# A decoder layer on one core: the first attention layer gets memory of its own, and the cross layer's loop begins beside it at its step 25 in place of 38

## The chip, the cores and the metric

The kernel runs on one core of one Trainium2 chip. The metric is the device time of one execution in microseconds (us), as the median of several runs. The engines are named as the profile names them: PE (TensorE; PEld is its weight load), DVE (VectorE), ACT (ScalarE), POOL (GpSimd) and SP (SyncE, here a queue of DMA issues).

## The reference, cut to what matters

Eight batches of 112 tokens and 512 columns go through three layers, each with a layer norm ahead of it and a residual sum behind it.

```python
x = x + _L0_attn_ref(_layernorm(x), Wqkv_w, Wqkv_b)    # 16 heads of 32, rotary, causal, scores in float32
x = x + _L0_xattn_ref(_layernorm(x), ctx_2048, ...)    # a second layer norm, values rounded to fp8 steps,
                                                       # 16 heads over x and 16 over ctx (375 rows), projection
x = x + _L0_ffn_ref(_layernorm(x), w_gate_up, w_proj)  # ternary weights, silu gate
```

Below, the first line is called the A layer. The second is called the cross layer; its first half is attention over x itself (halves S0 and S1 of eight heads each), its second half attention over the context (X0 and X1). The quantities of the A layer that matter here are, for each batch: q, k and v from one product with a bias, scores and softmax of four groups of four heads, and the product with v; then the two layer norms of the cross layer and four quantised copies of their result, which the cross layer's products read.

## The kernel before, in words

Everything is written out by hand. Each call `pe(...)`, `dve(...)`, `act(...)` or `pool(...)` appends one instruction to that engine's list with the semaphore values that it waits for, so the order of the calls in Python is the order of each engine's queue. Two step loops make those calls.

**The A layer's loop** is `run_a`, a generator of 53 steps. In a step it goes through `plan`, a list of stages with the step at which the first batch comes to them; a batch follows every 4 steps. The stages of a batch are: layer norm statistics `a_ln` and its scaling `a_h`, transposes `a_tr`, three products `a_mm` (L455, 12 matmuls each, one per step in three of four steps), addition of the bias on DVE `a_ev` (L467), rotary on POOL `a_rotary` (L481 to L487), transposes of q and k `a_tq` (L495) and their copies `a_te`. Then come the groups of four heads, one per step and four per batch: `a_s0` (scores L520 and L523 on PE, row maximum L529 on DVE, four exponentials L532 on ACT), `a_s2` (transposes L546) one step later, `a_s3` (product with v, L570) another step later, and `a_s4` (division and residual sum on DVE, L586 to L594). Last come the cross layer's two norms, `l_0` to `l_2` (L649 transposes), and `l_q` with `quant`: one multiplication, three short DVE instructions (L609 to L612) and two on POOL (L613, L614), four times for each batch. The norms' reciprocal roots are four small POOL instructions (L374 to L377). The lag between a batch's first step and its first head group is `A_LEAD`, 10.

**The cross layer's loop** is the `while tick < ...` loop at the end: item after item of `proj_items` (products `p_mm`, L806, 8 matmuls; for q and k then statistics `p_stats` on DVE, L386, roots on POOL, `lnb_z` on ACT, L746, and transposes L757), and 8 steps behind it the items of `att_items` (`t_s0` to `t_s6`; L896, L940 and L975 on PE, quantisation by `quant`, and the projection L1013 once per batch). Background stages `b_0` and `b_1` split the weights of the next half into a high and a low bf16 part; S1's begin at step 15. Each step of this loop begins with one further step of `run_a`, as long as there is one.

Before the change, 38 steps of `run_a` are emitted by themselves and the last 15 inside the cross layer's loop. S0's weights are split during the 38 (`s0prep`, one piece a step from step 3). The limit of 38 comes from memory: the two layers share places. The A layer keeps q and k in `aKV`, where the cross layer keeps its keys and values (`kS`, `vS`), keeps its bias, softmax and transposed softmax in the attention rings of the cross layer, and shares `zr` with it. The code hands the places over with `free_rings`, which makes the first use of a ring wait until all engines have come to a given point.

Eight PSUM banks go round in a pool, `bank`; four staging slots for weights go round in `st_ring`.

## Time and profile before

| | |
|---|---|
| median of 3 runs | 1350.96 us (1349.79 to 1355.85) |
| time of the profiled execution | 1349.61 us |
| its span | 1347.8 us |
| busy: PE, DVE, ACT, POOL | 1224.5, 977.8, 727.2, 826.1 us |
| share of the span | 91%, 73%, 54%, 61% |
| last A step emitted by itself ends, cross layer's first product starts | 215 us |

The page cuts the span into 40 slices of 33.7 us. The A layer fills the first six or so, and the cross layer's attention over x the next ones. PE's busy time is modelled at its end and counts slow matmuls as busy too, so it is read together with the granted clock.

### The profile page before, as it was taken

To read this page: it belongs to the slowest core of one execution; us is meant where nothing else is said; L and a number is where in the kernel's file an instruction comes from. 1 tells how busy PE (TensorE), PEld (TensorE's weight loads), DVE (VectorE), ACT (ScalarE), POOL (GpSimd) and SP (SyncE) were. 2 spreads that over 40 slices of the span, in tenths; PEclk is the share of its full clock that TensorE was granted. 3 is DMA by queue.
4 is the path that set the end of the run, shared out by engine and by line. 5 is a ranking of instruction groups with operands and counts; after the bars stand their busy time and mean duration, and the time that the engine had idled before them with its cause. 6 is when DMAs were issued, how large, how long until landed. Compare 5 with 4: busy or idle time off the path is not lost.

```text
span 1347.8 us, 19252 instructions
## 1 busy us (share of the span) xinstructions
PE 1224.5 (91%) x6411; PEld 832.4 (62%) x6432; DVE 977.8 (73%) x2826; ACT 727.2 (54%) x1936; POOL 826.1 (61%) x1106
## 2 busy tenths in 40 slices
PE   3999998679999999999999999998889887798998
PEld 1666666456667666677777777765556555455545
DVE  3557886689988887577776666599999999564241
ACT  3444444567766765565555555576567656551130
POOL 1747885886786777344444453379778878465271
PEclk8888887999999999999999999999999999798999
DMA  8211100002220221011111111112221220000000
GB/s 245 64 48 47 32 1 1 0 1 64 63 64 1 64 85 53 27 40 55 51 43 55 55 47 32 32 35 63 75 59 51 67 66 16 1 1 5 24 1 28
DMA packets 18835, 59.30 MB, mean 44 GB/s; under 512 B 2240, under 2 KB 2368, under 8 KB 18736
## 3 DMA queue, kind: packets, MB, share of 16 engines
q1 hardware_dynamic: 17152, 55.03, 13.3%
q10 hardware_dynamic: 1584, 3.05, 0.8%
q8 instruction: 51, 0.84, 0.3%
q14 instruction: 48, 0.39, 0.1%
HBM read 56.23 MB, written 1.84 MB: 43 GB/s over the span
## 4 chain that ended last, share of the span: by engine, by line
PE 55%; DVE 26%; POOL 11%; ACT 4%; issue 2%; DMA 1%; ACTq 0%; POOLq 0%; SPq 0%
PE ps L816 11%; PE ps L1080 7%; PE ps L1013 7%; PE ps L806 5%; PE ps L455 4%; DVE big L928 4%; PE ps L975 4%; PE ps L1129 4%; PE ps L908 4%; POOL big L375 3%; DVE big L352 3%; PE ps L940 2%; DVE big L386 2%; PE ps L523 2%; DVE big L353 2%
## 5 line engine op out<-in xcount | busy, mean ns | idle before, releaser
L816 PE MATMUL ps<-big 128*125 128x512 bf16 x1152 | 267.3, 382 | 1.3 <-ACT big L911 1.2
L746 ACT ACTIVATE big<-ps,big 112x128 f32<-112x128 f32 (+1 forms) x512 | 192.5, 458 | 88.4 <-POOL big L377 87.7
L816 PEld LDWEIGHTS ps<-big 128*125 128x125 bf16 x1152 | 156.9, 138 | 82.9 <-issue 2.2
L374 POOL TENSOR_SCALAR big<-big 112x4 f32<-112x4 f32 (+2 forms) x160 | 46.7, 292 | 259.8 <-DVE big L389 254.5
L806 PE MATMUL ps<-big 128*112 128x512 bf16 x768 | 184.4, 383 | 4.6 <-ACT big L746 1.9
L375 POOL TENSOR_TENSOR big<-big 112x4 f32<-112x4 f32 (+2 forms) x160 | 161.1, 1007 | 13.5 <-DMA big<-in_cst 0.2
L928 DVE TENSOR_SCALAR big<-big 112x112 f32<-112x112 f32 (+1 forms) x256 | 158.4, 639 | 6.8
L911 ACT ACTIVATE big<-ps,big 112x375 f32<-112x375 f32 x128 | 74.1, 579 | 147.9 <-DVE big L910 147.8
L613 POOL TENSOR_TENSOR big<-big 128x448 f32<-128x448 bf16 x96 | 99.7, 1038 | 69.3 <-DVE big L925 53.4
L806 PEld LDWEIGHTS ps<-big 128*112 128x112 bf16 x768 | 99.6, 131 | 67.0 <-issue 5.1
L386 DVE BATCH_NORM_STATS2 big<-ps 112x6 f32<-112x128 f32 (+1 forms) x512 | 113.1, 282 | 37.7 <-PE ps L816 32.8
L975 PE MATMUL ps<-big 125*128 125x224 f32 (+1 forms) x512 | 123.3, 364 | 11.5 <-ACT big L955 10.8
L614 POOL TENSOR_TENSOR big<-big 128x448 bf16<-128x448 f32 x96 | 120.9, 1259 | 7.5
L1013 PE MATMUL ps<-big 128*112 128x512 bf16 x512 | 115.9, 380 | 2.7 <-POOL big L377 1.3
L975 PEld LDWEIGHTS ps<-big 125*128 125x128 f32 (+1 forms) x512 | 93.4, 196 | 23.5 <-ACT big L955 13.9
L908 PE MATMUL ps<-big 128*112 128x375 f32 x256 | 104.8, 491 | 2.8 <-ACT big L955 2.8
L1080 PE MATMUL ps<-big 128*128 128x448 bf16 x512 | 98.3, 353 | 0.0
L455 PE MATMUL ps<-big 128*112 128x512 bf16 x288 | 84.2, 454 | 14.9 <-DVE big L242 13.9
L940 PEld LDWEIGHTS ps<-big 112*125 112x125 f32 (+1 forms) x512 | 79.4, 178 | 27.6 <-ACT big L341 3.3
L763 ACT ACTIVATE big<-ps,big 128x448 f32<-128x448 f32 (+1 forms) x128 | 96.0, 750 | 0.3 <-PE ps L757 0.3
L1013 PEld LDWEIGHTS ps<-big 128*112 128x112 bf16 x512 | 65.6, 130 | 47.5 <-issue 4.4
L940 PE MATMUL ps<-big 112*125 112x112 f32 (+1 forms) x512 | 86.3, 271 | 8.9 <-ACT big L341 4.3
(113 smaller groups left out, 2365.4 us busy)
## 6 DMA issues: line engine op xcount, KB each, us to landing
big<-in_ctx_t SPq DMA_DIRECT2D x32, 375.0 KB, 3.1
big<-in_w_s SPq DMA_DIRECT2D x16, 512.0 KB, 3.6
big<-in_w_p SPq DMA_DIRECT2D x16, 512.0 KB, 3.6
big<-in_w_x SPq DMA_DIRECT2D x16, 512.0 KB, 3.6
big<-in_w_g SPq DMA_DIRECT2D x16, 512.0 KB, 4.1
big<-in_w_d SPq DMA_DIRECT2D x8, 512.0 KB, 3.6
big<-in_w_a SPq DMA_DIRECT2D x8, 384.0 KB, 4.5
big<-in_x ACTq DMA_DIRECT2D x8, 224.0 KB, 8.6
```

Of the source, the lines that this page charges most:

```text
L375: t = pool(lambda e: e.tensor_tensor(r, r, cf[0:rows, C_HALF:C_HALF + n], ALU.pow), t, t_c)
L386: t = dve(lambda e, j=j: e.bn_stats(st[:, j, :], src[0:rows, width * j:width * j + width]), toks, free)
L455: t = pe(lambda e, k=k, s=s, w=w, n=n: e.matmul(bk[0:T, :], xT[:, s, k, :], wA[:, w, k, 512 * j:512 * j + 512], start=n == 0, stop=n == 11 ...
L746: t = act(lambda e, j=j: e.activation(z[0:rows, 128 * j:128 * j + 128], bk[0:rows, 128 * j:128 * j + 128], ACT.Identity, bias=rr[0:rows, 4 ...
L806: t = pe(lambda e, k=k, s=s, n=n: e.matmul(bk[0:T, :], xq[:, k, :], w[:, s, k, col:col + 512], start=n == 0, stop=n == 7), xq_tok[(v, b)], ...
L816: t = pe(lambda e, k=k, s=s, u=u, n=n: e.matmul(bk[0:CK, :], cT[:, s, k, CK * c:CK * c + CK], w[:, u, k, col:col + 512], start=n == 0, sto ...
L908: t = pe(lambda e: e.matmul(bk[0:T, 0:SC], q[:, h, :], kk[:, g, :], start=True, stop=True), bt["ready"], free)
L928: tl = dve(lambda e, j=j: e.tensor_scalar(hl[0:T, w * j:w * j + w], p[0:T, w * j:w * j + w], ri[:, j:j + 1], None, ALU.mult), tr, hf)
L940: t = pe(lambda e, j=j: e.transpose(bb[0:rows, T * j:T * j + T], hl[0:T, rows * j:rows * j + rows], identf[0:T, 0:T]), it["tl"], free, sig ...
L975: t = pe(lambda e, c=c: e.matmul(bk[:, o:o + 224], v[0:rows, c, 128 * g:128 * g + 128], pT[0:rows, 224 * c:224 * c + 224], start=c == 0, s ...
L1013: t = pe(lambda e, h=h, s=s, n=n: e.matmul(bk[0:T, :], cat[:, h, :], hf["wp"][:, s, h, :], start=n == 0, stop=n == 15), bt["tcat"], free, ...
L1080: t = pe(lambda e, k=k, s=s, n=n, bk=bk, which=which: e.matmul(bk[:, 0:448], wg[:, k, 2048 * which + 128 * m:2048 * which + 128 * m + 128] ...
```

## The change

Memory. The A layer gets places that nothing of the cross layer's first half uses. Its bias and one shared ring `az` go into staging slots 2 and 3, which the A layer borrows until its end (`a_lent`), so that only two staging slots are left for the weights meanwhile. q and k go into the last part of the ring for transposed softmax (`aPT`), which the cross layer's first half leaves free; the rest goes into two areas inside PW[0], behind the A layer's own weights. To fit, some rings lose a slot: v 3 to 2, softmax 3 to 2, q and k 2 to 1 each, and one slot `az` takes the place of `zr`, `zl` and the old `az`. The bias is no longer loaded from ACT's queue at the start but from SP's, behind the A layer's weights.

Order. `A_LEAD` is 9 in place of 10; in a step `a_s3` comes first, and the transposes of q and of k both come in the batch's step 8. `run_a` has 51 steps. The cross layer's loop begins after 25 of them (`A_T0`), so 26 are emitted inside it. S0's last 3 pieces of weights are split inside the loop; S1's begin at its step 12 in place of 15, its first 16 pieces waiting for the A layer's last product (`a_mid`) and the rest for its end (`a_end`).

```diff
-        ptr = Ring([f32(rings.take(672), 672) for _ in range(2)])
+        aPT = rings.take(1344)
+        ptr = Ring([f32(aPT + 672 * i, 672) for i in range(2)])
...
+            for i, toks in [s for s in st_ring.idle if s[0] >= 2]:
+                st_ring.idle.remove((i, toks))
+                a_lent.extend(toks)
+            return load(sync_items, a_bias[0:T, :], bias, s_bias, 16, a_lent)
...
-        zl = Ring([f32(PW[0] + 512 * i, 512) for i in range(2)])
-        az = Ring([f32(PW[0] + 2048, 512)])
-        fl = Ring([f32(PW[0] + 1024 + 512 * i, 512) for i in range(2)])
-        aw = Area(PW[0] + 6144, 6144)
-        ab = Area(aKV, 2432)
-        ac = Area(a_att, sz_att)
+        aw = Area(PW[0] + 6144, 2048)
+        au = Area(PW[0] + 8192, 4096)
-        a_bias = f32(ac.take(1536), 1536)
-        t_bias = load(act_loads, a_bias[0:T, :], bias, s_bias, 16)
+        a_bias = f32(aST[2], 1536)
+        az = Ring([f32(aST[2] + 1536, 512)])
...
-                 Ring([f32(aw.take(512), 512) for _ in range(3)])]
+                 Ring([f32(au.take(512), 512) for _ in range(2)])]
-        a_p = Ring([f32(a.take(448), 448) for a in (aw, ac, ac)])
+        a_p = Ring([f32(au.take(448), 448) for _ in range(2)])
+        a_qT = Ring([f32(aPT + 224, 448).rearrange("p (j t) -> p j t", j=4)])
+        a_kT = Ring([f32(aPT + 896, 448).rearrange("p (j t) -> p j t", j=4)])
...
-        A_LEAD, A_H, A_Q = 10, 4, 14
+        A_LEAD, A_Q = 9, 13
...
+                ("h", 2, a_s3),
+                (lead - 1, lambda it: a_tq(it, 0)),
+                (lead - 1, lambda it: a_tq(it, 1)),
...
-                (7, lambda it: a_tq(it, 0)),
-                (8, lambda it: a_tq(it, 1)),
...
-        for n in range(4 * NB + A_LEAD + A_H - 8):
+        A_T0 = 25
+        for n in range(A_T0):
...
-                prep_a()
+                t_bias.append(prep_a())
...
-        drain(s0prep)
-        free_rings((kS, vS, qr), a_all)
...
+        S1_AT = LEAD + 4
+        s1prep = prep_units("S1", PW[0], w_s[1], w_p[1], (0, 1, 2), lambda: a_mid)
+        for u in s1prep[16:]:
+            u["free"] = lambda: a_end
-        bg = {LEAD + 7: prep_units("S1", PW[0], w_s[1], w_p[1], (0, 1, 2), lambda: a_end),
+        bg = {S1_AT: s1prep,
...
+            next(s0prep, None)
             if next(tick_a, "end") == "end" and not a_end:
...
-            if tick == LEAD:
-                free_rings((catr, pr, hlr, ptr), all_now())
+            if A_T0 + tick == 4 * NB + 3:
+                a_mid.extend(all_now())
```

Three places in the queues show what moves. In the changed file the A layer's lines stand three further down: L455 is L458, L495 L498, L520 L523, L523 L526, L546 L549, L570 L573, ACT's L532 is L535; L649, L746, L757 and L806 stay.

PE, the queue around the cross layer's first products in the kernel before (L806), one row for each group of matmuls:

```order
L649 MATMUL ps<-big 128x112 x4
L546 MATMUL ps<-big 112x112 x4
L520 MATMUL ps<-big 112x448
L523 MATMUL ps<-big 112x112 x4
L570 MATMUL ps<-big 112x32 x4
L546 MATMUL ps<-big 112x112 x4
L520 MATMUL ps<-big 112x448
L523 MATMUL ps<-big 112x112 x4
L570 MATMUL ps<-big 112x32 x4
L806 MATMUL ps<-big 112x512 x8
L546 MATMUL ps<-big 112x112 x4
```

The same place of PE's queue with the change, from the first L806 of the cross layer on:

```order
L806 MATMUL ps<-big 112x512 x8
L573 MATMUL ps<-big 112x32 x4
L549 MATMUL ps<-big 112x112 x4
L523 MATMUL ps<-big 112x448
L526 MATMUL ps<-big 112x112 x4
L649 MATMUL ps<-big 128x112 x4
L806 MATMUL ps<-big 112x512 x8
L573 MATMUL ps<-big 112x32 x4
L549 MATMUL ps<-big 112x112 x4
L523 MATMUL ps<-big 112x448
L526 MATMUL ps<-big 112x112 x4
L458 MATMUL ps<-big 112x512 x12
```

Before, the cross layer's products come in when the A layer's own (L455) are over; now they alternate with the last seven of the A layer's (L458), and each of 16 head groups has one product of the cross layer beside it in place of 4. The product with v (L573) now stands ahead of the transposes (L549) in a step.

SP's queue at the start, the kernel before:

```order
L1251 DMA big<-in_w_a 128x768 x4
L1251 DMA big<-in_w_a 128x768 [waits s_dve,s_act] x4
L1251 DMA big<-in_w_s 128x1024 [waits s_dve,s_act] x4
L1251 DMA big<-in_w_s 128x1024 [waits s_dve] x4
```

and with the change:

```order
L1251 DMA big<-in_w_a 128x768 x4
L1251 DMA big<-in_w_a 128x768 [waits s_dve,s_act] x4
L1251 DMA big<-in_bias 112x1536 [waits s_act,s_dve]
L1251 DMA big<-in_w_s 128x1024 [waits s_dve,s_act] x2
L1251 DMA big<-in_w_s 128x1024 [waits s_dve] x6
```

The bias now waits for the splitting of the last weights that used slots 2 and 3, and the loads of S0's weights stand behind it.

ACT's queue at the first normalisation of the cross layer (L746) with the change:

```order
L535 ACTIVATE big<-ps,big 112x112 x4
L654 ACTIVATE big<-ps,big 128x112 x4
L746 ACTIVATE big<-ps,big 112x128 x4
L535 ACTIVATE big<-ps,big 112x112 x4
L746 ACTIVATE big<-ps,big 112x128 x4
L535 ACTIVATE big<-ps,big 112x112 x4
```

L746 and the exponentials L535 alternate as they did before in the last four head groups; now they do so for 16.

## Rows read from the trace of the kernel before

**Rows 1.** The page: PE's busy tenths and granted clock in 40 slices of 33.7 us.
```profile
PE   3999998679999999999999999998889887798998
...
PEclk8888887999999999999999999999999999798999
```
**Rows 2.** Timeline of PE before 141 us: start, duration, line, tiles, count.
```profile
135.21 0.55 PE L546 MATMUL ps<-big 112*112 112x112 f32 x4
...
137.65 2.78 PE L455 MATMUL ps<-big 128*112 128x512 bf16 x12
140.26 0.55 PE L435 MATMUL ps<-big 112*128 112x112 f32 x4
...
141.31 1.03 PE L523 MATMUL ps<-big 32*112 32x112 f32 x8
```
**Rows 3.** Timeline of PE: the cross layer's first product, a steady step, step 26.
```profile
215.27 3.19 PE L806 MATMUL ps<-big 128*112 128x512 bf16 x8
...
316.45 1.89 PE L806 MATMUL ps<-big 128*112 128x512 bf16 x8
318.18 0.36 PE L940 MATMUL ps<-big 112*112 112x112 f32 x2
...
319.16 1.89 PE L806 MATMUL ps<-big 128*112 128x512 bf16 x8
...
335.82 1.89 PE L806 MATMUL ps<-big 128*112 128x512 bf16 x8
```
**Rows 4.** Busy time, clock and DMA in four stretches of the span.
```profile
core 0: us, PE busy (x) PEld busy (x) DVE busy (x) ACT busy (x) POOL busy (x), PEclk, DMA share, GB/s
139.00:215.00 76.00, 69.40 (x395) 52.64 (x393) 60.76 (x114) 32.99 (x135) 60.22 (x75) 0.77 0.05 15
215.00:241.00 26.00, 22.02 (x124) 16.14 (x124) 17.18 (x59) 12.34 (x46) 16.63 (x27) 0.81 0.00 1
241.00:291.00 50.00, 31.08 (x182) 20.76 (x181) 38.00 (x142) 29.78 (x84) 43.91 (x68) 1.00 0.00 1
291.00:336.00 45.00, 41.86 (x246) 29.29 (x245) 42.46 (x158) 32.29 (x97) 32.74 (x48) 1.00 0.16 48
```
**Rows 5.** The same columns: head groups without products, and a steady batch.
```profile
196.00:215.00 19.00, 17.61 (x87) 14.84 (x86) 12.69 (x29) 8.11 (x34) 11.11 (x17) 0.54 0.01 2
...
316.60:333.20 16.60, 15.77 (x94) 11.02 (x92) 15.80 (x59) 12.18 (x36) 11.66 (x17) 1.00 0.22 66
```
**Rows 6.** Waits from 240 to 291 us: total us, times, longest.
```profile
ACT big L746 <- POOL big L377: 18.0, 8, 4.0
```
**Rows 7.** POOL's longest root instruction, 240 to 291 us: count, busy us, mean ns.
```profile
L375 POOL TENSOR_TENSOR big<-big 112x4 f32<-112x4 f32 x8 | 8.3, 1042 | 0.7
```
**Rows 8.** Timeline: two row maxima of DVE that follow one another.
```profile
224.58 0.59 DVE L529 TENSOR_REDUCE big<-ps 112x4 f32<-112x448 f32 x1
...
234.14 0.62 DVE L529 TENSOR_REDUCE big<-ps 112x4 f32<-112x448 f32 x1 [4.13 <-PE ps L523]
```
**Rows 9.** Line L610 on DVE from 47 to 215 us: ns min/median/max.
```profile
L610 DVE TENSOR_SCALAR big<-big x17: 276/277/1233, 114.4 to 210.3; 128x448 bf16<-128x448 bf16 x17
```
**Rows 10.** Timeline of PE: the wait of a step without a product ahead of it.
```profile
120.98 0.60 PE L546 MATMUL ps<-big 112*112 112x112 f32 x4 [1.57 <-ACT big L532]
```
**Rows 11.** Timeline of DVE at the start, and DMA issues (KB each, us to landing).
```profile
16.49 0.22 DVE L224 CAST big<-big 128x112 bf16<-128x112 f32 x1 [9.32 <-DMA big<-in_cst]
...
25.95 1.93 DVE L242 TENSOR_TENSOR big<-big 128x768 bf16<-128x768 f32 x2 [0.30 <-ACT big L241]
...
29.56 0.69 DVE L467 TENSOR_TENSOR big<-ps,big 112x512 f32<-112x512 f32 x1 [0.86 <-PE ps L455]
...
big<-in_w_s SPq DMA_DIRECT2D x16, 512.0 KB, 3.6
...
big<-in_bias ACTq DMA_DIRECT2D x1, 672.0 KB, 11.9
```
**Rows 12.** DVE's splitting of S1's weights, 316.6 to 333.2 us: busy us, mean ns.
```profile
L324 DVE SCALAR_TENSOR_TENSOR big<-big 128x512 bf16<-128x512 f32 x4 | 3.0, 742 | 0.0
```

More of the change, by code:

```diff
@@ L247, in decoder_layer @@
         ready = {}
+        a_lent = []
         def prep_a():
@@ L586, in a_s4 @@
             t = dve(lambda e: e.reciprocal(ri, sm[0:T, 16:32]), g["te"])
-            ring, after = (zr, None) if b < 5 else (az, marks["a_mm"])
-            zi, z, zf = ring.take()
+            zi, z, zf = az.take()
             t2 = dve(lambda e: e.tensor_tensor(
                 z[0:T, :].rearrange("p (h d) -> p h d", h=16), bk[0:T, :].rearrange("p (h d) -> p h d", h=16),
-                ri.unsqueeze(2).broadcast_to([T, 16, 32]), ALU.mult), t, it["tpv"], zf, after)
+                ri.unsqueeze(2).broadcast_to([T, 16, 32]), ALU.mult), t, it["tpv"], zf, a_lent)
             bank.release(bi, t2)
@@ L624, in l_0h @@
             si, rr, tr, _ = it["st"]
-            it["zr"], it["fr"] = (zr, fr) if b < 4 else (zl, fl)
-            after = marks["a_mm"] if b >= 4 else None
-            zi, z, zf = it["zr"].take()
+            zi, z, zf = az.take()
             th = act(lambda e: e.activation(z[0:T, :], x1[0:T, b, :], ACT.Identity, bias=rr[0:T, 1:2],
-                                            scale=rr[0:T, 0:1]), tr, zf, x1tok[b], after)
+                                            scale=rr[0:T, 0:1]), tr, zf, x1tok[b])
             small.release(si, th)
@@ L650, in l_2 @@
                                                   identf[0:T, 0:T]), th, free, signal=k == 3)
-            it["zr"].release(zi, t)
-            fi, f, ff = it["fr"].take()
+            az.release(zi, t)
+            fi, f, ff = fr.take()
             for k in range(4):
@@ L669, in l_q @@
             if last:
-                it["fr"].release(fi, t1)
-        A_LEAD, A_H, A_Q = 10, 4, 14
+                fr.release(fi, t1)
+        A_LEAD, A_Q = 9, 13
         def run_a():
@@ L688, in run_a @@
                 ("h", 1, a_s2e),
-                (7, lambda it: a_te(it, 0)),
-                (8, lambda it: a_te(it, 1)),
+                (lead - 1, lambda it: a_te(it, 0)),
+                (lead - 1, lambda it: a_te(it, 1)),
                 (4, lambda it: a_rotary(it, 0)),
                 (5, lambda it: a_rotary(it, 1)),
-                ("h", 2, a_s3),
-                (lead + 8, l_0),
-                (lead + 9, l_1),
-                (lead + 10, l_2),
-                (lead + 11, lambda it: l_q(it, (0,), False)),
-                (lead + 12, lambda it: l_q(it, (1,), False)),
-                (lead + 13, lambda it: l_q(it, (2,), False)),
-                (lead + 14, lambda it: l_q(it, (3,), True)),
+                (lead + 7, l_0),
+                (lead + 8, l_1),
+                (lead + 9, l_2),
+                (lead + 10, lambda it: l_q(it, (0,), False)),
+                (lead + 11, lambda it: l_q(it, (1,), False)),
+                (lead + 12, lambda it: l_q(it, (2,), False)),
+                (lead + 13, lambda it: l_q(it, (3,), True)),
                 (5, lambda it: a_mm(it, 2)),
@@ L705, in run_a @@
                 (0, a_h),
-                (lead + 9, l_1h),
-                (lead + 8, l_0h),
+                (lead + 8, l_1h),
+                (lead + 7, l_0h),
             ]
@@ L1164, in decoder_layer @@
             if n == 2:
-                prep_a()
+                t_bias.append(prep_a())
             if n >= 3:
                 next(s0prep, None)
-        drain(s0prep)
         def all_now():
             return [Tok(q.sem, q.count) for q in (pe, dve, act, pool)]
-        a_all, a_end = all_now(), []
-        def free_rings(which, toks):
-            for r in which:
-                for i in range(len(r.slots)):
-                    r.free[i] = list(toks)
-        free_rings((kS, vS, qr), a_all)
+        a_mid, a_end = [], []
         pitems = proj_items()
@@ L1209, in decoder_layer @@
         while tick < n_items + LEAD + 12:
+            next(s0prep, None)
             if next(tick_a, "end") == "end" and not a_end:
-                assert tick <= LEAD + 7
+                assert tick < S1_AT + 16
                 a_end.extend(all_now())
-            if tick == LEAD:
-                free_rings((catr, pr, hlr, ptr), all_now())
+                st_ring.release(2, *a_end)
+                st_ring.release(3, *a_end)
+            if A_T0 + tick == 4 * NB + 3:
+                a_mid.extend(all_now())
             for kind, lag, f in order:
```

13 lines of the change are left out of this document (6 added, 7 removed).

## The prediction

> **What bounds the kernel now.** I read the page's slices first, then PE's timeline to find the steps, then busy time by stretch, then the waits. The slices show PE near full in the A layer, but with a granted clock of 0.8; behind it the clock is near 1 [rows 1]. So in the A layer PE is busy because it is slow.
>
> To price the change I need the stretch in which the two kernels differ. With lag 9 the changed kernel starts its cross layer at A step 25, with the 17th of 32 head groups. Before, that group's scores start at 141.3 us, with one A product more done than the change will have done; a product takes 2.61 us at full clock, from 137.65 to 140.26 [rows 2]. So the new start answers to about 139 us of before. The A layer now ends with the cross layer's step 25, and before, step 26 begins at 335.8 us [rows 3]. From there on both have the same work left. **The change is decided in these 197 us**, which become 26 steps.
>
> The kernel before spends them so [rows 4]: 12 A steps alone in 76 us (6.3 each), 4 head groups beside the cross layer's first products in 26 us (6.5 each), 11 steps with only the A layer's tail in 50 us (4.6 each), 11 steps of cross layer alone in 45 us (4.1 each). DVE's busy time adds up to 60.8 + 17.2 + 38.0 + 42.5 = 158.4 us, POOL's to 60.2 + 16.6 + 43.9 + 32.7 = 153.5. PE has to be put at full clock. A head step is 5.05 us with a product (135.21 to 140.26) and 2.44 without [rows 2]; a cross product is 1.73 from start to start, the attention matmuls beside it 0.98 [rows 3]; a set of transposes is 0.4, a projection two products' length. So 16 x 2.44 + 7 x 2.61 + 12 x 0.4 for the A layer and 26 x 1.73 + 19 x 0.4 + 18 x 0.98 + 2 x 3.46 for the cross layer: about 139 us. No engine has work for over 81% of the 197 us, while a steady batch has DVE busy 15.80 and PE 15.77 of 16.60 us, 95% both [rows 5]. **The slack is 197 - 158 = 39 us at the very most.**
>
> **The change, part by part.**
>
> *The steps beside each other.* In steps 0 to 8 there are nine head groups, seven A products, nine cross products and some ten sets of transposes: 62 us of PE at full clock, 6.9 per step. POOL has 5.0 per A step (60.2 / 12) [rows 4], and new roots of about 2 us, half of it L375 [rows 7], in three steps of four: 6.5. DVE has 5.1 (60.8 / 12) and about 1 of statistics, an estimate: 6.1. Besides, there is a path from step to step. ACT's normalisation L746 waits for POOL's roots, 18.0 of 51 us [rows 6]; the exponentials stand behind L746 on ACT, PE's next scores behind those. The four steps that have both in the trace average 6.5, with no A product in them, so I put this path at about 7. With PE's 6.9, the path's 7 and POOL's 6.5 so close together I take **7.8** per step, in which PE works 88%: between the 80% that DVE and POOL reach in the A layer and the steady 95%. In steps 9 to 11 the A products are gone and attention fills; the path remains: **7.3**. In steps 12 to 15 DVE carries heads and tail (12.7 us in 3.6 steps, 3.5 each) and a full cross step with weight splitting (15.8 / 4 = 3.95) [rows 5], 7.45: **8.0**. In steps 16 to 25 the heads are gone, and what is left of DVE's 158 after 55 + 18 + 30 is 5.5 per step: **6.3**. Together 9 x 7.8 + 3 x 7.3 + 4 x 8.0 + 10 x 6.3 = 187 us in place of 197: **-10 us**. Its bounds are 167 (DVE at 95%) and 215 (below).
>
> *The clock.* From 196 to 215 us PE runs head groups without products, is busy 17.6 of 19 us and gets 0.54 of its clock, near the lower of its levels of 1.2 and 2.4 GHz [rows 5]. From 241 on, with a cross product in every step, it gets 1.00 although it is busy 62% [rows 4]. With the change every head group from the 17th on has such a product beside it, so the slow stretch should go. That is inside the 187, since PE is summed at full clock there.
>
> *The order inside an A step.* A step without a product ahead of it makes PE wait 1.57 us for exponentials [rows 10], with the product with v and one set of q or k transposes already between. The transposes now go to another step, so I charge 0.4 us for each of four such steps in the part that still runs alone: **+1.6 us**, between 0 and 4.
>
> *The start.* The bias leaves ACT's queue, where its load took 11.9 us beside the constants for which DVE waits 9.32 us until 16.49; the splitting of the A weights stands behind that on DVE [rows 11]. At the pace of S0's loads (512 KB in 3.6 us) its 672 KB are 4.7 us of traffic. I take **-1 us**, between -4.7 and +1, as most of the queue is other loads. What speaks for +1: the bias now goes out when the last A weights are split (25.95 + 1.93 = 27.9) and needs some 4.7 us, and it is first read at 29.56 [rows 11], so that the first bias additions come 3 us late. PE has two more A products of 2.6 us queued then, which cover it. S0's loads stand behind the bias and come some 4 us later; ACT waits in its queue for the first, under the same cover.
>
> *Two staging slots.* A load has near two steps, 12 us alone and more in the loop, and lands in 3.6 [rows 11]: nothing. *One slot for q, for k and for `az`*: each is released, by an instruction ahead in the order, in the step in which it is taken again or before: nothing, and what is not nothing lies in the 88%.
>
> *S1's weights three steps earlier.* Three pieces of 0.74 us on DVE [rows 12] are done before step 26 and fall away behind it, where DVE is 95% busy: **-2 us**, between -3 and 0. `a_mid` and `a_end` name points two steps back: nothing.
>
> Sum: -10 + 1.6 - 1 - 2 = -11.4 us against the profiled execution's 1349.6 (span 1347.8): 1338.2. The median of the runs stood 1.35 us above that execution, so **1339.5 us**. A measurement can tell about 0.5%, 6.8 us.
>
> **A rule beside the rows.** L610 on DVE takes 277 ns as a median and up to 1233 ns in the A layer [rows 9], where POOL's rotary and quantisation run beside it. The Trainium skill (SBUF — State Buffer, "Who interferes with whom") says that such a DVE instruction and a POOL instruction lock one port pair against each other, each for its full length. The trace agrees. The sum takes DVE's present stretching as it stands; what more of it would do is priced in the last rival.
>
> **The rivals.**
>
> *DVE alone is the bound*, as in the steady batch: 158.4 / 0.95 = 167 us, -30, in all 1320 us. For it: a path of 7 us is hidden once steps are long. Against: three engines within 15% of each other in steps 0 to 8, and DVE at 76% from 241 to 291 us.
>
> *No gain that shows.* The path over POOL and ACT sets the step in both kernels, and DVE stays at its present 80%: 158.4 / 0.80 = 198 us, in all 1345 to 1353. For it: the wait of L746. This is also what comes if the cross layer's work is queued earlier but runs no earlier; against that, its products stand in every step of PE's queue.
>
> *Slower: POOL and DVE hold each other up.* With 6.5 us of POOL in each of 16 head steps, L610 and its two like would stand behind POOL more often. If all three took the longest time, DVE would have 3 x 0.96 = 2.9 us more per step, 9.0 in place of 6.1, and the step would be 9.5. One step of before was like that: 224.58 to 234.14 us, with 4.13 of waiting for PE [rows 8]. Then 16 x 9.5 + 63 = 215 us, +18, in all 1367 us. It decides from 8.4 us per head step on, where 16 x 8.4 + 63 = 197. Against it: the four such steps average 6.5, and L610's median is its short time.
>
> **How the numbers follow.** Forecast, with its own range of 1331 to 1344: 0.42. DVE bound: 0.20. No gain: 0.26. Slower: 0.12. The likeliest gives 1339.5. The range goes from 1318, which takes in the DVE case, to 1356, past the no-gain case; what is outside is most of the slower case and a few in a hundred below. Faster by over 0.5% are forecast and DVE case, 0.62; within 0.5% the third, 0.26; slower 0.12.
>
> **What the new profile would show.** The first L806 near 138 us and step 26's near 325; head groups in the cross layer about 7.8 us apart; a granted clock of 1.0 from the first L806 on; DVE about 85% busy in between; the bias landing before 33 us. It is wrong if the first L806 comes later than 143 (the start or the single slots), if steps 0 to 15 take over 8.4 us on average (path or port), or if DVE is over 92% busy there (a gain of 20 us and more).

## The result: slower by 1.5%, and the profile after

| | before | changed |
|---|---|---|
| median of the runs | 1350.38 us (1349.59 to 1355.85, 4 runs) | 1371.57 us (1371.22 to 1372.54, 4 runs) |
| ratio, 95% interval | | 1.0149 [1.0122, 1.0177] |
| profiled execution, span | 1349.6, 1347.8 us | 1371.79, 1370.0 us |

Forecast were 1339.5 us in a range of 1318 to 1356. The measured time lies above the range, on the side to which 0.12 had been given. The page of the changed kernel, whose slices answer to [rows 1]:

```profile
span 1370.0 us, 19279 instructions
...
PE 1240.3 (91%) x6432; PEld 836.1 (61%) x6432; DVE 986.5 (72%) x2826; ACT 726.5 (53%) x1936; POOL 824.0 (60%) x1106
...
PE   3897899777899999999999999998889898799998
...
PEclk9897789889999999999999999999999999799999
```

Two of PE's events place the difference, the first L806 and step 26, which stand at 215.27 and 335.82 in [rows 3]. PE's timeline of the changed kernel (start, duration):

```profile
153.15 1.89 PE L806 MATMUL ps<-big 128*112 128x512 bf16 x8
...
354.44 1.93 PE L806 MATMUL ps<-big 128*112 128x512 bf16 x8 [0.36 <-ACT big L903]
```

| stretch | before | forecast | changed |
|---|---|---|---|
| start to the first L806 (before: to the point that answers to it) | 139 | 138 | 153.2 |
| from there to step 26 | 197 | 187 | 201.3 |
| step 26 to the end | 1012.0 | 1010 | 1015.6 |

So the 22 us come in three parts: **14 before the two layers meet, 4 while they run beside each other, 4 behind step 26**. The forecast's own terms give 139 + 1.6 - 1 = 139.6 for the first, where its list of signs said "near 138"; against the terms the parts are 14, 14 and 6. All this compares two single executions, and that of before is among its faster ones (1349.61, where the medians of before lie between 1350.38 and 1353.75), so each part is uncertain by a few us. The merged steps by stretch, with the A layer's second half ahead of them (window, its length, busy time of PE, PEld, DVE, ACT and POOL, granted clock, DMA share, GB/s):

```profile
core 0: us, PE busy (x) PEld busy (x) DVE busy (x) ACT busy (x) POOL busy (x), PEclk, DMA share, GB/s
99.80:153.10 53.30, 45.08 (x264) 33.04 (x263) 39.03 (x69) 22.67 (x82) 34.42 (x48) 0.81 0.12 37
153.10:233.40 80.30, 71.08 (x400) 50.59 (x398) 54.48 (x136) 38.58 (x135) 60.15 (x88) 0.85 0.05 14
233.40:258.30 24.90, 19.94 (x124) 14.66 (x121) 18.94 (x65) 15.74 (x64) 13.46 (x24) 0.86 0.00 1
258.30:291.90 33.60, 25.13 (x156) 18.47 (x157) 27.31 (x88) 20.51 (x69) 22.25 (x35) 0.89 0.06 17
291.90:354.40 62.50, 47.45 (x236) 30.78 (x236) 60.39 (x177) 32.57 (x95) 53.74 (x62) 0.89 0.14 43
```

These are steps 0 to 8 (8.9 us each, forecast 7.8), 9 to 11 (8.3 and 7.3), 12 to 15 (8.4 and 8.0), 16 to 25 (6.3 and 6.3). DVE's busy time adds up to 161.1 us (forecast 158), POOL's to 149.6, PE's to 163.6: none over 82% of 201 us. The clock stays at 0.85 to 0.89, where 1.0 was forecast.

**The start.** SP's queue, DVE, ACT and PE around the first head group (before the brackets as above; in brackets, the idle time of the engine ahead of the row and what ended it):

```profile
27.46 0.34 SPq L1251 DMA_DIRECT2D big<-in_bias  x1
...
33.61 0.69 DVE L470 TENSOR_TENSOR big<-ps,big 112x512 f32<-112x512 f32 x1 [5.44 <-DMA big<-in_bias]
...
34.59 0.72 ACT L319 ACTIVATE big<-big 128x512 bf16<-128x512 f32 x1 [8.22 <-DMA big<-in_w_s]
...
49.94 0.35 PE L523 MATMUL ps<-big 112*112 112x448 bf16 x1
```

The bias landed at about 33.6 us, DVE was idle 5.4 us for it, and the first scores (the small matmuls behind this L523) started at 50.2 us, 2.8 later than before (47.4).

**Two steps of the A layer ahead of the first L806, 8.1 and 7.5 us long.** POOL, ACT and PE from 118.9 to 132.2 us; L490 ends the rotary embedding, L380 to L383 are the roots of the A layer's normalisations, L628 and L640 apply them, L535 are the exponentials, L649 the transposes of the normalised batch:

```profile
118.93 1.26 POOL L490 TENSOR_TENSOR big<-big 112x512 f32<-112x512 f32 x1
...
120.27 0.21 POOL L380 TENSOR_SCALAR big<-big 112x1 f32<-112x1 f32 x1
...
122.02 0.23 POOL L383 TENSOR_SCALAR big<-big 112x1 f32<-112x1 f32 x1
...
122.29 0.81 ACT L628 ACTIVATE big<-big 112x512 f32<-112x512 f32 x1 [4.19 <-POOL big L383]
...
123.53 0.33 ACT L535 ACTIVATE big<-ps,big 112x112 f32<-112x112 f32 x1
...
125.44 0.97 PE L573 MATMUL ps<-big 112*112 112x32 f32 x8 [2.51 <-ACT big L559]
...
127.47 1.78 POOL L490 TENSOR_TENSOR big<-big 112x512 f32<-112x512 f32 x1
...
129.33 0.21 POOL L380 TENSOR_SCALAR big<-big 112x1 f32<-112x1 f32 x1
...
131.29 0.81 ACT L640 ACTIVATE big<-big 112x512 f32<-112x512 f32 x1 [5.47 <-POOL big L383]
...
132.15 1.01 PE L649 MATMUL ps<-big 112*128 112x112 f32 x4 [4.07 <-ACT big L640]
```

The normalisations were due at `lead + 8` with a lead of 10; they are now due at `lead + 7` with a lead of 9, two steps of the loop earlier. Steps repeat their pattern every four, with the batch: the normalisations' steps used to be those without a rotary embedding, and now are the two that have one. POOL works on the rotary embedding for 4.3 to 4.9 us of such a step; the roots stand behind it in POOL's queue, ACT's L628 and L640 wait for them, the exponentials stand behind those in ACT's queue, and PE, in a step without an A product, waits for both. That makes the batch from L438 at 122.38 to the next at 152.76 take 30.4 us. Before needs 24.3 us for the batch of the same number (L435 at 116.01 and 140.26) and 26.9 for the next. The waits of 92 to 153 us, of which before has 4.8 us for L640 and, among its larger ones, none for L649 (us in all, times, longest):

```profile
ACT big L628 <- POOL big L383: 9.5, 3, 4.2
ACT big L640 <- POOL big L383: 7.5, 2, 5.5
...
PE ps L649 <- ACT big L640: 5.1, 2, 4.1
```

### The profile page after: what moved, and what is told of

Same layout as the page of the kernel before. It is cut to its first block, busy times and chain, and to the rows that moved or that the text cites. A ratio compares the mean times of both kernels' runs of the same rounds, so it can differ in the third digit from the quotient of the medians.

```text
span 1370.0 us, 19279 instructions
## 1 busy us (share of the span) xinstructions
PE 1240.3 (91%) x6432; PEld 836.1 (61%) x6432; DVE 986.5 (72%) x2826; ACT 726.5 (53%) x1936; POOL 824.0 (60%) x1106
## 4 chain that ended last, share of the span: by engine, by line
PE 52%; DVE 26%; POOL 13%; ACT 4%; issue 3%; DMA 1%; ACTq 0%; POOLq 0%; SPq 0%; DVEq 0%
PE ps L816 11%; PE ps L1080 7%; PE ps L1013 6%; PE ps L806 6%; DVE big L928 4%; PE ps L975 4%; PE ps L1129 4%; PE ps L908 3%; POOL big L381 3%; DVE big L358 3%; DVE big L392 2%; PE ps L940 2%; PE ps L458 2%; PE ps L757 2%; ACT big L746 2%
## 5 line engine op out<-in xcount | busy, mean ns | idle before, releaser
L816 PE MATMUL ps<-big 128*125 128x512 bf16 x1152 | 270.2, 385 | 0.6 <-ACT big L911 0.6
L746 ACT ACTIVATE big<-ps,big 112x128 f32<-112x128 f32 (+1 forms) x512 | 192.5, 458 | 111.1 <-POOL big L383 110.3
L806 PE MATMUL ps<-big 128*112 128x512 bf16 x768 | 192.8, 396 | 12.5 <-ACT big L746 7.7
L380 POOL TENSOR_SCALAR big<-big 112x4 f32<-112x4 f32 (+2 forms) x160 | 45.8, 286 | 250.9 <-DVE big L395 244.5
L381 POOL TENSOR_TENSOR big<-big 112x4 f32<-112x4 f32 (+2 forms) x160 | 164.6, 1029 | 13.6 <-DMA big<-in_cst 0.4
L806 PEld LDWEIGHTS ps<-big 128*112 128x112 bf16 x768 | 102.8, 136 | 80.0 <-issue 12.7
L975 PE MATMUL ps<-big 125*128 125x224 f32 (+1 forms) x512 | 125.4, 369 | 16.3 <-ACT big L955 10.8
L1013 PE MATMUL ps<-big 128*112 128x512 bf16 x512 | 118.6, 386 | 2.5 <-ACT big L903 2.2
L458 PE MATMUL ps<-big 128*112 128x512 bf16 x288 | 85.1, 456 | 17.5 <-DVE big L243 12.7
L1013 PEld LDWEIGHTS ps<-big 128*112 128x112 bf16 x512 | 66.6, 132 | 49.1 <-issue 7.6
L957 DVE COPY big<-ps 112x224 f32<-112x224 f32 (+1 forms) x128 | 54.5, 426 | 54.3 <-PE ps L940 54.3
```

The source lines that it names most:

```text
L381: t = pool(lambda e: e.tensor_tensor(r, r, cf[0:rows, C_HALF:C_HALF + n], ALU.pow), t, t_c)
L458: t = pe(lambda e, k=k, s=s, w=w, n=n: e.matmul(bk[0:T, :], xT[:, s, k, :], wA[:, w, k, 512 * j:512 * j + 512], start=n == 0, stop=n == 11 ...
L746: t = act(lambda e, j=j: e.activation(z[0:rows, 128 * j:128 * j + 128], bk[0:rows, 128 * j:128 * j + 128], ACT.Identity, bias=rr[0:rows, 4 ...
L806: t = pe(lambda e, k=k, s=s, n=n: e.matmul(bk[0:T, :], xq[:, k, :], w[:, s, k, col:col + 512], start=n == 0, stop=n == 7), xq_tok[(v, b)], ...
L816: t = pe(lambda e, k=k, s=s, u=u, n=n: e.matmul(bk[0:CK, :], cT[:, s, k, CK * c:CK * c + CK], w[:, u, k, col:col + 512], start=n == 0, sto ...
L975: t = pe(lambda e, c=c: e.matmul(bk[:, o:o + 224], v[0:rows, c, 128 * g:128 * g + 128], pT[0:rows, 224 * c:224 * c + 224], start=c == 0, s ...
```

## The experiments

Seven theories were in play; the letters are those of the expectations. **Phase** (P): the normalisations fall on the rotary's steps. **Bias** (B): it comes late. **Memory** (M): single slots and two staging slots. **Banks** (K): the cross layer's early products hold PSUM banks that the heads need. **Merging** (O): the early start itself costs. **v first** (S): the product with v at the head of a step makes PE wait for DVE. **The L746 path** (L): roots, L746 and exponentials set the pace of the merged steps. Ratios are against the kernel before in runs beside each; its medians were 1351.84, 1351.82, 1353.75 and 1351.13 us in the four groups e1 to e4, e5 to e8, e9 to e12 and e13 to e16.

| | base and edit | median us | ratio [95%] | first L806 | step 26 |
|---|---|---|---|---|---|
| e1 | change, norms 2 steps later | 1364.94 | 1.0087 [1.0059, 1.0115] | 147.4 | 343.3 |
| e2 | change, start 38 | 1382.47 | 1.0217 [1.0186, 1.0248] | 248.1 | 368.6 |
| e3 | change, bias early | 1365.56 | 1.0119 [1.0075, 1.0163] | 149.9 | 350.6 |
| e4 | before, norms 2 steps earlier | 1369.95 | 1.0124 [1.0095, 1.0152] | 234.7 | 353.9 |
| e5 | change, own banks | 1382.16 | 1.0225 [1.021, 1.024] | 153.9 | 365.6 |
| e6 | e1 + e3 + own banks | 1362.13 | 1.0094 [1.0067, 1.0121] | 140.6 | 344.7 |
| e7 | e1 + e3, start 38 | 1360.80 | 1.0071 [1.0056, 1.0086] | 222.7 | 345.6 |
| e8 | e1 + e3 | 1361.32 | 1.0073 [1.0058, 1.0088] | 142.2 | 339.1 |
| e9 | e8, v product last | 1359.58 | 1.0044 [1.0028, 1.006] | 144.0 | 337.6 |
| e10 | e9, start 38 | 1355.75 | 1.0016 [1.0005, 1.0028] | 219.7 | 342.7 |
| e11 | e9, start 32 | 1360.68 | 1.0054 [1.0038, 1.0069] | 191.2 | 347.9 |
| e12 | before, v product first | 1373.84 | 1.0152 [1.0137, 1.0168] | 235.3 | 359.5 |
| e13 | e9, L746 a step later | 1357.37 | 1.0031 [1.0014, 1.0048] | 145.9 | 337.0 |
| e14 | e13, start 38 | 1363.75 | 1.0081 [1.0051, 1.0111] | 220.0 | 346.7 |
| e15 | before, L746 a step later | 1351.78 | 0.9997 [0.9979, 1.0014] | 213.3 | 337.5 |
| e16 | change, L746 a step later | 1376.59 | 1.0165 [1.0125, 1.0204] | 154.4 | 361.7 |

(Before itself: 215.3 and 335.8.)

### e1: the normalisations two steps later

The edit moves all the normalisation and quantisation of the A layer's tail by two steps, so that it meets the steps without a rotary embedding again; a buffer of `a_h1` takes the place of `az` in `a_s4`, and the last of S1's early weights wait two steps longer.

```diff
-        A_LEAD, A_Q = 9, 13
+        A_LEAD, A_Q = 9, 15
...
-                (lead + 7, l_0),
-                (lead + 8, l_1),
...
+                (lead + 9, l_0),
+                (lead + 10, l_1),
...
-            zi, z, zf = az.take()
+            zi, z, zf = a_h1.take()
```

> The changed kernel with the two norms of the A layer's tail and the quantisation two steps later, so that they no longer fall on the steps in which POOL does the rotary (the sum's z goes through the slot of the first norm to keep one slot for each). Theory P (phase: the norms' roots stand behind the rotary on POOL, ACT's exponentials behind the norms): the part of the A layer that runs alone gets back to about 25 us per batch in place of 30, first product of the cross layer at 143 us in place of 153, and the merged steps gain too: 1350 to 1362 us. Theory M (memory: single slots, two staging slots): unchanged, 1369 to 1374. Theory O (overlap itself: the merged steps are full): at most 2 us better.

It measured 1364.94 us, 6.6 below the change (8.4 by the ratios), a smaller gain than the 1350 to 1362 us expected of the phase, and a larger one than its rivals allow. ACT still has waits for the roots, but shorter, and PE's wait at L649 is no longer among the larger ones of 92 to 153 us:

```profile
ACT big L640 <- POOL big L383: 7.1, 2, 3.7
...
ACT big L628 <- POOL big L383: 3.9, 2, 2.0
```

The first L806 came 5.8 us earlier, and step 26 another 5.4 us: steps 0 to 8 of the merged loop took 73.3 us in place of 80.3, and the rest of it 1.6 more. PE's row for steps 0 to 8:

```profile
147.39:220.71 73.32, 65.50 (x396) 46.60 (x394) 49.98 (x132) 36.85 (x129) 59.14 (x83) 0.91 0.05 15
```

The phase is one cause, with 7 to 8 of the 21 us. What the edit gains by step 26 it does not keep wholly: behind step 26 this kernel has 1363.7 - 343.3 = 1020.4 us, 5 more than the change, since the tail now reaches past that step.

### e4: the same phase in the kernel before

```diff
-                (lead + 8, l_0),
-                (lead + 9, l_1),
...
+                (lead + 6, l_0),
+                (lead + 7, l_1),
...
```

The quantisation moves with them, and one more batch, the fifth, takes its buffers from the first pair of rings.

> The kernel before, with nothing changed but the two norms and the quantisation of the A layer's tail two steps earlier, so that they fall on the rotary's steps as they do in the changed kernel. Theory P: four or five batches of the alone part take 30 us in place of 25.5: 1365 to 1375 us. Theories M and O: no difference, 1349 to 1353.

It measured 1369.95 us, 18 above before. Its first L806 is 19.4 us late and its step 26 18.1. The same chain of rows appears, in a kernel that has before's memory, before's bias and before's start of the cross layer:

```profile
149.41 1.26 POOL L487 TENSOR_TENSOR big<-big 112x512 f32<-112x512 f32 x1
...
150.75 0.72 POOL L374 TENSOR_SCALAR big<-big 112x1 f32<-112x1 f32 x1
...
152.47 1.21 POOL L377 TENSOR_SCALAR big<-big 112x1 f32<-112x1 f32 x1
...
153.72 0.81 ACT L640 ACTIVATE big<-big 112x512 f32<-112x512 f32 x1 [5.74 <-POOL big L377]
...
154.59 1.01 PE L649 MATMUL ps<-big 112*128 112x112 f32 x4 [4.75 <-ACT big L640]
```

So the phase alone can cost 18 us; the batches of 116.86 to 146.85 and to 176.87 take 30.0 us each where before has 24.3 and 26.9. Here the loss stands wholly in the part of the A layer that runs alone. In the change (against e1) it is 5.8 us there, 5.4 in the merged steps, and 4.8 less behind step 26.

### e3: the bias from ACT's queue again

Three pieces of 512 words, in places that the first A steps leave free, loaded where before loaded it; the cross layer waits for these places at its steps 8 and 12, and the merged layout is otherwise kept.

```diff
-        a_bias = f32(aST[2], 1536)
+        a_bias = [f32(a_att + 2688, 512), f32(a_att + 1792, 512), f32(aKV + 1920, 512)]
+        for j in range(3):
+            t_bias0 = load(act_loads, a_bias[j][0:T, :], bias[:, 512 * j:512 * j + 512], s_bias, 16 * (j + 1))
```

> The changed kernel with the bias loaded at the start from ACT's queue again, in three pieces into places that the cross layer uses only after the A layer's last bias addition. In the changed kernel DVE waited 5.4 us for the bias. Theory B (the late bias costs what the first head group is late): first scores at about 46 us in place of 50.2, and 3 to 5 us less in all, 1366 to 1369. If the loss is taken up later by waits of the alone part: no difference, 1370 to 1373.

It measured 1365.56 us (1363.69 to 1374.53, 5 runs), 6.0 below the change and 4.1 by the ratios. Taken by itself this is not clear of the noise (the intervals of e3 and of the change overlap), but e8 below has the same edit on top of e1, with 3.6 us by the medians and 1.9 by the ratios. The first scores start at 45.31, 4.9 us earlier than in the change and 2.1 earlier than before:

```profile
45.31 1.03 PE L528 MATMUL ps<-big 32*112 32x112 f32 x8
```

### e2, e7, e10, e11: the start of the cross layer alone

```diff
-        A_T0 = 25
+        A_T0 = 38
```

> The changed kernel, but with the cross layer begun after 38 steps of the A layer, as before the change; memory, order and lags are those of the change. Theory P: the alone part loses 5 us at the start and 5 us for each of about five batches whose norms meet a rotary: 1368 to 1380 us, so that the earlier start by itself was a gain or neutral. Theory O: without the 13 further merged steps it is back near the time before, 1350 to 1357. Theory M: between, with waits for ring slots in the alone part.

In the change's own schedule, going back to step 38 made it slower still, 1382.47 (expected were up to 1380): **there the early start was worth 11 us** (9 by the ratios), against the theory that merging is what costs.

> Norms later and bias early, but the cross layer begun after 38 steps as before the change. What is left of the change then is the memory (single slots, two staging slots), lag 9 and the order inside a step. If these cost nothing: 1349 to 1353 us. If theory M holds in part: 1356 and more. Against the next kernel it gives what the 13 further merged steps are worth: in the changed kernel's own schedule they were a gain of 11 us.

> Norms later and bias early at start 25. If the two gains add up: 1357 to 1361 us.

With phase and bias mended the two starts came out equal, 1360.80 and 1361.32. The two mends nearly add up: 1371.57 - 6.6 - 6.0 is 1359.0, e8 has 1361.32.

> The same with the cross layer begun after 38 steps. Theory S: all that is left of the change is its memory and lag 9, so the time before comes back, 1349 to 1354 us. Theory M: 1357 to 1361. Against the kernel ahead of it, it gives the worth of the earlier start with nothing else in the way: if my forecast of the overlap was right in kind, the earlier start is 5 us or more faster; if the merged steps are full, it is the same within 3 us or slower.

> The same with the cross layer begun after 32 steps, between the two. If the worth of a merged step is steady, it lies between the two within 3 us; if only the first steps with A products and heads beside the cross layer are too full, it is the fastest of the three.

The expectation for e7 had been 1349 to 1353, or 1356 and more if memory cost something; e10 shows that 5 us of the 1360.80 go with the place of the v product and its slot.

With the v product last as well, the late start is better, 1355.75 against 1359.58, and step 32 is no optimum between, 1360.68. So the worth of the early start goes from +11 over 0 to -4 us as the schedule of the A layer is mended: an early start helps where the steps that run alone are bad. The -4 is only just clear of the noise, and against it stood a forecast gain of 10. e10 has the change's memory (but for a third slot of v and the bias's place) and its lead of 9 with before's start, and stands 2 us above the kernel before: single slots for q, k and `az`, two staging slots and the shorter lead cost next to nothing, as forecast. Its 1355.75 lie between what the two theories in its expectation allowed.

### e5, e6: banks of their own

Two PSUM banks are set aside for the cross layer's products in its first 28 steps, six for all else.

```diff
+        pbank = Pool(bank.slots)
+        pbank.idle = [bank.idle.pop(0), bank.idle.pop(0)]
+        own[0] = pbank
```

> The changed kernel, but in the cross layer's first 28 steps its products use two PSUM banks of their own and everything else the other six, so that no matmul of another stage takes a bank that the normalisation L746 still holds. In the changed kernel PE waited for L746 some 15 us in the merged steps, though most of its instructions read nothing that L746 writes. Theory K (banks): these waits go, 1360 to 1367 us. Theory P alone (the exponentials behind the norms on ACT set the pace): the waits move to the next instruction and the time stays within 2 us of 1371.

> Changed kernel with the norms two steps later, the bias loaded early and the banks of their own, all three. If their gains add up (6.6 and 6.0 measured, banks 4 to 10): 1350 to 1356 us. If theory K is wrong: about 1359.

1382.16 us, 10.6 above the change, and that in the merged steps (211.7 us from the first L806 to step 26 in place of 201.3); on top of the two mends, 1362.13 against 1361.32 without. The banks, divided this way, do not help; another division was not tried.

### e9, e12: the product with v in its old place

e9 puts `a_s3` back behind the other head stages, with a third slot for v in the lent staging area. So e9 by itself can't tell the order from the slot. e12 moves only the order, the other way, in the kernel before.

```diff
-                ("h", 2, a_s3),
...
+                ("h", 2, a_s3),
```

> Norms later and bias early (1361.3), and besides the product with v back at its old place, last of the head stages in a step, with a third slot for v in the staging memory that the bias has left. Theory S (with the product with v first, PE's step begins with a matmul that needs DVE's copy from the end of the step before, 13.9 us of waiting in the alone part): 1352 to 1358 us. Theory M (single slots, two staging slots): 1360 to 1362.

> The kernel before, with nothing changed but the place of the product with v, first in a step as in the change. Theory S: 1355 to 1361 us. Theory M: 1350 to 1353.

e12 measured 1373.84 us, 20 above before and far past its expectation of 1355 to 1361. Its first L806 stands at 235.29 where before has 215.27, 20.0 of the 25.3 us between the two profiled spans; 3.6 more come up to step 26. In the change the place is worth less: by the ratios 3.9 us between e8 and e9 (with 1359.58, e9 lies between its two theories), 7.4 between e7 and e10. While the A products still run it costs nothing in the change's schedule (in e12 10.3 us, L435 at 177.40 for 167.15): e7 transposes the seventh batch at 168.41 (L440) where e10 has 171.48 (L441), and e8 reaches the first L806 1.8 us before e9. e7 then loses 6 us up to its own first L806, in the head groups that have no A product beside them; e9 gains its 3.4 us between the first L806 and step 26. The mechanism is best seen where head groups run alone, in e7 (L575 is the product with v, L563 DVE's copy of the transposed softmax, L534 the row maximum, L528 the scores):

```profile
198.23 1.83 PE L528 MATMUL ps<-big 32*112 32x112 f32 x8
...
200.10 0.62 DVE L534 TENSOR_REDUCE big<-ps 112x4 f32<-112x448 f32 x1 [0.62 <-PE ps L528]
...
202.85 0.61 DVE L563 COPY big<-ps 112x448 f32<-112x448 f32 x1
...
203.51 1.70 PE L575 MATMUL ps<-big 112*112 112x32 f32 x8 [3.45 <-DVE big L563]
...
207.81 1.83 PE L528 MATMUL ps<-big 32*112 32x112 f32 x8
...
209.68 0.62 DVE L534 TENSOR_REDUCE big<-ps 112x4 f32<-112x448 f32 x1 [3.96 <-PE ps L528]
...
210.22 0.61 DVE L563 COPY big<-ps 112x448 f32<-112x448 f32 x1
...
210.89 1.70 PE L575 MATMUL ps<-big 112*112 112x32 f32 x8 [0.31 <-DVE big L563]
```

PE's step begins with a matmul that needs DVE's copy. On DVE that copy stands behind the row maximum, which needs the scores, PE's last group of the step before. So PE waits 3.45 us for DVE ahead of 203.51, and DVE 3.96 us for PE behind it. The next step, 7.4 us to 210.89, has hardly a wait of PE (0.31) and is long because its matmuls are slow. PE is busy for 7.07 of these 7.38 us at a granted clock of 0.50, the lower level: 1.70 us for L575, which took 0.97 at 196.56. With the v product last, scores and copy have PE's other groups between them. In e12's waits of 92 to 153 us the same shows as DVE's wait for the scores, of which before has 6.6 us there. What PE's product with v waits for here is ACT's copy L556, the other engine that copies the transposed softmax:

```profile
DVE big L529 <- PE ps L523: 17.4, 7, 5.7
...
PE ps L570 <- ACT big L556: 5.6, 2, 2.9
```

### e13 to e16: L746 a step later

```diff
-                 ("p", 3, p_t), ("b", 3, b_2), ("a", 1, t_s1), ("p", 1, p_z), ("a", 8, t_s6),
+                 ("p", 3, p_t), ("b", 3, b_2), ("a", 1, t_s1), ("p", 1, z_soon), ("p", 2, z_late), ("a", 8, t_s6),
```

`z_late` is `p_z` for the first 24 products of the cross layer, `z_soon` for the rest.

> The all-mended kernel at start 25 (1359.6) with the cross layer's normalisation on ACT (L746) one step later for its first 24 products, so that POOL has a step's time for the roots and the exponentials don't stand behind a wait for them. Theory L: the merged steps get shorter by 0.5 us or more each, 1340 to 1352 us. Theory of full engines: within 3 us of 1359.6; a held PSUM bank more could also make it slower, as with the banks of their own.

> The same at start 38 (1355.8 without it). Theory L: a smaller gain, as only 15 steps are merged and few have heads: 1348 to 1354 us, so that the early start now wins against it. Full engines: 1353 to 1358.

> The kernel before with that one edit. Theory L: ACT waited 18 us for the roots in 51 us; some 5 us of it are gained, 1344 to 1349. Full engines: 1350 to 1354.

> The changed kernel itself with that one edit. Theory L: 1358 to 1367. If the norms behind the rotary hold the same queue up anyway: 1369 to 1373.

The step's delay gave 2 us on e9 (1357.37, within the noise), cost 8 on e10 (1363.75) and left before as it was (1351.78, ratio 0.9997); the change came out 5 higher (1376.59), with an interval that holds the change's own 1.0149. For e14 and e16 neither theory had allowed that. A path on which L746 alone sets the pace would have moved all four the same way. The forecast had put such a path at 7 us beside PE's 6.9 and POOL's 6.5. It is not what holds the merged steps, or not by itself.

None of the sixteen was faster than the kernel before.

## Why the prediction was wrong

Three steps of the sum failed. The order of the stages was priced at 1.6 us and cost some 11 to 12 (phase 7 to 8, e1; v product 4, e9). The bias's lateness was taken to be covered and was not. And the merge was to save 10 us at a clock of 1.0, where the clock stayed at 0.85 to 0.89 and the stretch grew by 4; with all mends the early start still costs 4 (e9 against e10).

**The start (forecast -1, bounds -4.7 to +1).** Measured by e3, the bias from SP's queue costs 4 to 6 us, and 2 to 4 once the phase is mended (e1 to e8). The text had the cost in hand, 3 us late on DVE, and covered it with "PE has two more A products of 2.6 us queued then". The cover did not hold: the first scores start 2.8 us later than before, and 4.9 later than with the bias on ACT's queue. The addition is on the path to the first head group, which nothing precedes.

**The order inside an A step (forecast +1.6, bounds 0 to +4).** This is the largest error in kind. Looked at were the transposes that moved, priced by instructions moved; not looked at were two things whose instructions all stay the same. First, the lead went from 10 to 9 and the lag behind it from 8 to 7, together two steps on a pattern of four, so the roots fell behind the rotary embedding (e1: 7 to 8 us, e4: 18). Second, the product with v came first in its step, which ties PE's step to DVE's copy (e12: 20 in the kernel before, 4 here by e8 and e9, and none of these 4 ahead of the first L806). The stretch to the first L806 took 14 us more than the 139 of before; e8, with phase and bias mended, has 10.9 of them back, and 3 stay open. It was known to be wrong from 143 us on, as the text had said of "the start or the single slots". The slots were nearly innocent (e10).

**The clock and the 187 us (forecast -10, measured +4).** The failing sentence is "since PE is summed at full clock there", with its forecast of a clock of 1.0 from the first L806 on. In the terms of that sum: 62 us of PE work for steps 0 to 8 were worth 6.9 us a step, and PE was taken to be 88% busy, 7.8. (The 62 is itself a slip: 9 x 2.44 + 7 x 2.61 + 9 x 1.73 + 10 x 0.4 are 59.8.) Measured were 71.08 us of PE, 7.9 a step, and a share of 71.08 / 80.3 = 89%, 8.9. The share was right, the work was about right (71.08 x 0.85 = 60.4), the clock was not. The same holds over the whole stretch. Before, the four windows of [rows 4] have 69.40 x 0.77 + 22.02 x 0.81 + 31.08 + 41.86 = 144 us of PE at full clock; after, 71.08 x 0.85 + 19.94 x 0.86 + 25.13 x 0.89 + 47.45 x 0.89 = 142. Both busy sums are 164 us: the stretch of 0.54 [rows 5] did go, but the 95 us that had run at 1.00 went with it, to 0.85 to 0.89. So the merge gave PE nothing.

The clock is not a cause that stands by itself, though. e1 moves nothing but the normalisations, and its steps 0 to 8 take 73.3 us with the same work (65.50 x 0.91 = 59.6) and the same share (89%), at 0.91 in place of 0.85. So 7.0 of the 10 us by which these steps missed their forecast of 70.2 go with the phase, and 5.6 of the 7.0 are busy time of PE, which means clock. No run held the clock fixed: whether the waits lower the clock or both have a further cause is not shown. Steps 9 to 15 were 4.6 us over for another reason, as PE is busy 75 to 80% there. No mend took that back: these seven steps take 58.4 us in the change, 61.1 in e1, 61.9 in e8, 59.2 in e9, 64.7 with banks of their own (e5) and 56.4 in e13, where 53.9 were forecast. What holds them stays open. Steps 16 to 25 took exactly the forecast 6.3.

e9 is the best trial of the early start, with all the mends. PE's busy time and clock over its merged steps and the steps behind them, and the latter of e10 and of before:

```profile
144.00:219.70 75.70, 68.69 (x413) 48.29 (x411) 52.60 (x141) 38.18 (x135) 60.20 (x87) 0.91 0.04 12
219.70:337.57 117.87, 92.08 (x501) 65.63 (x500) 104.42 (x321) 69.04 (x221) 90.78 (x123) 0.86 0.09 28
337.00:365.00 28.00, 22.73 (x115) 14.72 (x114) 24.54 (x83) 16.31 (x52) 21.63 (x31) 0.88 0.24 76
```

```profile
342.00:362.00 20.00, 19.19 (x117) 13.63 (x115) 18.98 (x73) 15.40 (x48) 14.67 (x22) 1.00 0.19 57
```

```profile
335.00:355.00 20.00, 19.19 (x118) 13.69 (x116) 19.10 (x72) 15.33 (x46) 13.87 (x21) 1.00 0.20 67
```

e9's 26 merged steps take 193.6 us, 3.4 less than before's stretch of 197, and behind step 26 it pays 1357.3 - 337.6 = 1019.7 us in place of 1012.0: its A layer's tail still runs there, POOL is 77% busy where e10 has 73%, and the clock is 0.88 where e10 and before have 1.00. Its four steps from 26 to 30 take 24.3 us, e10's 16.6. What the merge saves in one place comes back behind it.

**S1's weights earlier (forecast -2).** Behind step 26 the change has 3.6 us more, not 2 less: the step from 26 to 27 takes 10.8 us where before has 7.0. The earlier splitting itself gives nothing that shows: e10 splits its last pieces in step 28, as the change does, where before goes on to step 32, and its tail ends as before's does; behind step 26 it has 1354.6 - 342.7 = 1011.9 us, where before has 1012.0. The step of the sum that failed is "fall away behind it, where DVE is 95% busy": fewer pieces on DVE did not shorten that stretch. The 3.6 us more are then the early start's, and 3.2 of them lie in steps 26 to 30 (19.9 us in place of 16.6).

**The nearest rival** forecast 1367 us and +18 for the slower side, and the steps 0 to 15 averaged 8.7 us, past its 8.4. But its mechanism is not the one at work. DVE's instructions that would be held up by POOL kept their short time as a median (ns, least, median and longest):

```profile
L612 DVE TENSOR_SCALAR big<-big x26: 276/278/1222, 110.8 to 295.9; 128x448 bf16<-128x448 bf16 x26
```

and DVE's busy time rose by 2.7 us over the whole stretch, from 158.4, where the rival needed 2.9 in every step. The rule of the Trainium skill (SBUF — State Buffer, "Who interferes with whom") that such a pair excludes each other is borne out by single instructions: the one of 1222 ns starts at 124.86 beside POOL's L484, which runs from 124.31 to 125.95, and ends 0.14 us behind it. It is worth at most about those 3 us here.

**What was right**: steps 16 to 25, DVE's load, POOL's, PE's work at full clock, the cost of memory. "No gain that shows" described the merged steps' length best, 201 us against its 198, and e9's 194; but its ground, the wait of L746, is what e13 to e16 do not bear out, so the nearness is partly luck.

The causes one behind the other, by the ratios: from 1.0149 to 1.0073 phase and bias (e8; 10.3 us), to 1.0044 the v product (e9; 3.9), to 1.0016 the early start itself (e10; 3.8), and the last 2.2 us what e10 still has of the change, memory and lead above all. Each ratio is uncertain by 2 to 4 us, so the order of size of the later steps is shown and not their figures.

## What to carry to other kernels

When a lead or a lag changes, write down for each engine which stages of the periodic pattern now share a step, and in which order they stand in its queue: a shift by two steps changes no instruction and cost up to 18 us. A stage that opens an engine's step should not need what the other engine makes from that engine's last group of the step before. And before idle engines are filled by merging two phases, put the busiest engine's work at the clock that its present busy stretches get, not at the clock of the stretch in which it idles: here 0.77 to 0.81 and 1.00 before, and 0.85 to 0.89 came.

## What the runs showed of the hardware

PE's mean granted clock changed little with how the two layers were laid over each other. From 45 us to the 31st cross step it is 0.88 before (268.19 us busy in 307.46), 0.87 with the change (278.33 in 329.30), 0.87 in e9 (272.24 in 316.85), 0.86 in e10 (277.30 in 314.30). The lowest are those of kernels that take longest there: 0.84 in e12 (282.08 in 331.10), e2, e5 and e16, 0.83 in e4. Inside that, single stretches went from 0.54 (before, head groups without a product) to 1.00 (cross layer alone). With a product of the cross layer beside them the slow head groups ran at 0.85 in the change and 0.91 in e1, and the cross layer's own stretch no longer had its 1.00. That a low clock and a long stretch go together is what the runs show; which of them brings the other is not.
